# Last stage of a four-layer kernel: the running state and its product with the query in halves of two PSUM banks

## The chip, the cores and the metric

The kernel runs on one core of a Trainium2 chip. The metric is the device time of one execution in microseconds (us). Three runs of the kernel before gave 3492.67 to 3494.13 us, with a median of 3493.6 us. Engines are called PE (TensorE, the matrix engine), DVE (VectorE), ACT (ScalarE), POOL (GpSimd) and SP (SyncE, which issues DMAs here).

## The reference

Four layers follow one another on x of shape (16, 64, 32, 32), each as `x = x + layer(gn(x))`. Only the fourth is touched. For each image n its 65,536 values form a sequence s, and with A = 4 channels:

```python
q, k, v = in_proj_weight * x + in_proj_bias        # each n, s, A
q = softplus(q); k = softplus(k)
s = cumsum(k[:, :, :, None] * v[:, :, None, :], axis=1)
z = cumsum(k, axis=1)
numer = einsum('nsi,nsij->nsj', q, s)
denom = einsum('nsi,nsi->ns', q, z)[:, :, None]
y = numer / denom                                  # then shifted by one position
y = sum(hid_proj_weight * y, -1) + hid_proj_bias
y = sum(out_proj_weight * tanh(y), 1) + out_proj_bias
```

## The kernel before

The program has four stages, one per layer, that follow one another with a barrier between. The last is `layer3`. It takes one image after the other (B = 16, here called batches). The sequence of an image lies on 128 partitions by 512 columns (HALF), so one running sum over the sequence is a product with a lower triangle `tri` of ones within each column, plus what all columns before add up to, which is kept in `carry`.

Per batch there are five running sums, called terms: that of k (term 0, index A) and those of k*v_j for j = 0 to 3 (terms 1 to 4). Each term has four components i, and each component fills one PSUM bank of 512 float32 values per partition. So `p_state` has four banks, and it is there once; `p_sum` has two banks, `p_turn` and `p_out` one each, which makes all eight.

PE makes a term in `state(b, n)`: four products with `tri` (L1251), then four short ones (L1256) that add the carry of component i, which lies on its own 32 partitions ("lane"). The records of the trace have two entries for each such product of float32 values. DVE multiplies the four banks by the query in one operation, `times_query` (L1139), into one of two buffers `prod`. PE then transposes and adds the four components of `prod` into `p_sum` (`sum_terms`, L1271, sixteen transposes). From there DVE takes the reciprocal for term 0 (`denominator`, L1145) and `y` for the others (`divide`, L1151). After that the four products with the hidden weights (DVE L1161, PE L1282 and L1287), tanh on ACT (L1084), the gate on POOL (L1033) and the output (PE L1295 and L1301, one batch late) follow.

Each engine has an order written out by hand, in its own `main(b, u, left)`, and the engines meet in semaphores alone. PE's order in a batch is: `turn` of the next batch, `state` 0, `output` of the batch before, `state` 1, sum 0, `state` 2, sum 1, `state` 3, sum 2, `state` 4, sum 3, sum 4, then `totals` of the next batch (L1242, products with `pick`), then `hidden` four times. DVE puts work on the next batch's inputs between its five products: `project` (L1108), `lost_part` (L1113, written to `expo`), `relu_log` (L1117), `keys_x_values` (L1123, written to `kv`, a view of `xt`). ACT works on `expo` and `lift` (L1056 to L1064), POOL on the biases and the end of the softplus (L1015, L1019).

Two semaphores tie the terms. `state_ready` counts terms that PE has finished; DVE waits for it in `times_query`. `queried` counts products that DVE has finished; PE waits for it at the start of `state`, since the four banks are written anew, and in `sum_terms`. The batch before the first and the two last batches are written apart (`over_batches`); `left` is 0 in the last batch, which prepares no other.

Of the kernel before, what the change touches and what calls it, by code (L numbers as in the profile page):

```python
# [7 lines left out]
ALU = mybir.AluOpType  # L8
# [6 lines left out]
HALF = H * W // 2  # L15
# [869 lines left out]
def layer3(nc, xt, d, out, early, row_stats):  # L885


    A = ATT
    TERMS = A + 1
    LOCAL = TERMS + A  # L890
    LANE = 32
    tiles, early_in = early
    inw, inb = (tiles[name] for name in EARLY)
    with ExitStack() as ctx:
        def sb(name, shape, dt=F32):
            return ctx.enter_context(nc.sbuf_tensor(name + "_3", shape, dt))

        def pb(name, shape):
            return ctx.enter_context(nc.psum_tensor(name + "_3", shape, F32))

        def sem(name):
            return ctx.enter_context(nc.semaphore(name + "_3"))
# [6 lines left out]
        query = [sb(f"query{n}", [P, A, HALF]) for n in range(2)]  # L909
        expo, lift = sb("expo", [P, A, HALF]), sb("lift", [P, A, HALF])  # L910
        hidw = [sb(f"hidw{n}", [P, A, HALF]) for n in range(2)]
        prod = [sb(f"prod{n}", [P, A, HALF]) for n in range(2)]
# [3 lines left out]
        carry = sb("carry", [P, HALF + 1])  # L916
# [6 lines left out]
        p_state = pb("p_state", [P, A, HALF])  # L923
# [18 lines left out]
        state_ready = sem("state_ready"); queried = sem("queried"); summed = sem("summed")  # L942
# [5 lines left out]
        def known(b):  # L948
            return isinstance(b, int)
# [146 lines left out]
        def _(dve):  # L1096
            tt, stt = nc.vector.tensor_tensor, nc.vector.scalar_tensor_tensor
# [30 lines left out]
                                             op0=ALU.add, op1=ALU.bypass).then_inc(carry_ready, 1)  # L1128

            def times_query(b, u, n):  # L1130
                dve.wait_ge(state_ready, b * TERMS + (n + 1))
                if n == 0:
                    dve.wait_ge(soft, b * 2 + 2)
                if n < 2:
                    if not (known(b) and b == 0):
                        dve.wait_ge(hid_summed, b * A + (n - 1))
                else:
                    dve.wait_ge(summed, b * TERMS + (n - 1))
                tt(prod[(u + n) % 2][:], p_state[:], query[u][:], ALU.mult).then_inc(queried, 1)  # L1139

            def denominator(b, u):
                dve.wait_ge(summed, b * TERMS + 1)
# [20 lines left out]
            def main(b, u, left):  # L1163
                if left:
                    dve.wait_ge(x_turned, b + 2)
                    project(value, 2, v_scaled)
                times_query(b, u, 0)
                if left:
                    project(key, 1, k_scaled)
                    project(query[1 - u], 0, q_scaled)  # L1170
                times_query(b, u, 1)
                denominator(b, u)
                if left:
                    lost_part(b + 1, 0)
                times_query(b, u, 2)
                divide(b, u, 0)
                if left:
# [39 lines left out]
        def _(pe):  # L1217
# [13 lines left out]
            def term(j, i):  # L1231
                return key[:, i] if j == A else kv[:, j, i]
# [12 lines left out]

            def state(b, n):
                j = (n + A) % TERMS
                if not (known(b) and b == 0 and n == 0):
                    pe.wait_ge(queried, b * TERMS + n)
                for i in range(A):  # L1250
                    nc.tensor.matmul(p_state[:, i], tri[:], term(j, i), start=True, stop=False)  # L1251
                if n == 0:
                    pe.wait_ge(carry_ready, b + 1)
                for i in range(A):
                    lane = slice(i * LANE, (i + 1) * LANE)
                    last = nc.tensor.matmul(p_state[:, i], give[lane, j], carry[lane, 0:HALF], start=False, stop=True)  # L1256
                last.then_inc(state_ready, 1)

            def sum_terms(b, u, n):
                pe.wait_ge(queried, b * TERMS + (n + 1))  # L1260
                if n < 2:
                    if not (known(b) and b == 0):
                        pe.wait_ge(tanh_ready, b * A + (n - 1))
                elif n == 2:
                    pe.wait_ge(recip_ready, b + 1)
                else:
                    pe.wait_ge(y_ready, b * A + (n - 2))
                r = (u + n) % 2
                for k in range(4):
                    for i in range(A):  # L1270
                        last = nc.tensor.matmul(p_sum[r][:, k * P:(k + 1) * P], prod[r][:, i, k * P:(k + 1) * P], ident[:],  # L1271
                                                start=(i == 0), stop=(i == A - 1), is_transpose=True)
                last.then_inc(summed, 1)
# [31 lines left out]
            def main(b, u, left):  # L1305
                if left:
                    turn(b + 1)
                state(b, 0)
                if not (known(b) and b == 0):
                    output(b - 1)  # L1310
                for n in range(1, TERMS):
                    state(b, n)
                    sum_terms(b, u, n - 1)
                sum_terms(b, u, A)
                if left:
                    totals(b + 1, (A, 0, 1, 2, 3)).then_inc(totalled, 1)
                for a in range(A):
                    hidden(b, u, a)
# [110 lines left out]
```

## Time and profile before

| | |
|---|---|
| median of three runs | 3493.6 us (3492.67 to 3494.13) |
| the profiled execution | 3487.4 us, its span 3485.6 us |
| mean granted TensorE clock over the span | 0.722 of full |
| busy over the span: PE, DVE, ACT, POOL | 1637.2, 1815.1, 761.0, 1754.7 us |
| instructions | 32244 |

The last stage begins at about 2320 us of the span, with its batches from 2404 us on. Times of a row are in microseconds from the span's start, or durations. PE records show when products stream; the ends are modelled, so two groups that follow one another can overlap a little, and the distance between two starts is the better measure.

### The profile page before, as it was taken

Reading aid. Unit: us, or ns where it says so; the run is one execution under the profiler, and the core shown is the slowest. Engines: PE = TensorE matmul, PEld = TensorE weight load, DVE = VectorE, ACT = ScalarE, POOL = GpSimd, SP = SyncE. Lnnn points to the kernel's source line nnn. Section 1 sums busy time; section 2 is a strip of 40 time slices with the busy share of each in tenths; the row PEclk is TensorE's granted clock in tenths of the full one; section 3 lists DMA queues with packets and bytes.
Section 4 is the critical chain, followed back from the end, with each engine's and each line's share of the span. In section 5 each row is a group of like instructions: output and inputs, shape, how many; then the busy total and the mean of one; then the engine's idle time right before and its main releaser. Section 6 shows DMA issues by size and latency. Waiting matters only on the chain. (4 is left out here: it accounts for less than half of the span.)

```text
span 3485.6 us, 32244 instructions
## 1 busy us (share of the span) xinstructions
PE 1637.2 (47%) x12432; PEld 974.3 (28%) x12432; DVE 1815.1 (52%) x1717; ACT 761.0 (22%) x893; POOL 1754.7 (50%) x1342
## 2 busy tenths in 40 slices
PE   3666321321313123141231412634888878888887
PEld 2455210110101001010010100431455445445545
DVE  3222432441616326153262534555888887788885
ACT  3111211101102011010111100523433432343341
POOL 0000067576675757757577574044355445535542
PEclk9878655665656556565565655776989999998999
DMA  7999533232332323323233232221131122113212
GB/s 315 431 431 432 234 92 102 71 107 86 95 104 72 108 78 103 103 71 109 77 104 103 72 109 65 85 78 38 58 108 65 57 81 90 57 57 105 67 55 82
DMA packets 118313, 414.64 MB, mean 119 GB/s; under 512 B 24802, under 2 KB 59764, under 8 KB 101108
## 3 DMA queue, kind: packets, MB, share of 16 engines
q1 hardware_dynamic: 62964, 262.86, 19.9%
q0 software_dynamic: 55296, 151.07, 14.1%
q8 instruction: 35, 0.57, 0.1%
q14 instruction: 18, 0.15, 0.0%
HBM read 396.78 MB, written 17.05 MB: 119 GB/s over the span
## 5 line engine op out<-in xcount | busy, mean ns | idle before, releaser
L441 POOL DMA_INDIRECT gath<-table,idx x1152 | 1162.4, 1009 | 561.0 <-issue 347.3
L568 DVE TENSOR_TENSOR gath<-gath,p_stat 128x2304 f32<-128x2304 f32 x128 | 326.4, 2550 | 749.0 <-DMA gath<-table,idx 260.0
L646 PE MATMUL p_col<-ident,taps 128*128 128x128 f32 x512 | 116.4, 367 | 705.8 <-issue 533.8
L495 ACT ACTIVATE cols<-p_col 128x512 f32<-128x512 f32 x128 | 75.2, 597 | 1240.5 <-remote 827.8
L646 PEld LDWEIGHTS p_col<-ident,taps 128*128 128x128 f32 x512 | 77.8, 184 | 751.7 <-issue 744.5
L1251 PE MATMUL p_state<-xt,tri 128*128 128x512 f32 x512 | 257.4, 650 | 64.5 <-DVE prod L1139 64.5
L1019 POOL TENSOR_TENSOR query<-query,expo 128x2048 f32<-128x2048 f32 x16 | 102.1, 6382 | 334.7 <-DVE query L1117 334.7
L1139 DVE TENSOR_TENSOR prod<-p_state,query 128x2048 f32<-128x2048 f32 x80 | 183.0, 2288 | 127.5 <-PE p_state L1256 127.5
L595 PE MATMUL p_conv<-sides,wconv 128*32 128x512 f32 x192 | 70.4, 893 | 330.7 <-ACT rows L466 330.7
L1287 PE MATMUL p_sum<-ident,prod 128*128 128x128 f32 x1024 | 174.0, 341 | 104.0 <-DVE prod L1161 104.0
L1161 DVE TENSOR_TENSOR prod<-hidw,y 128x2048 f32<-128x2048 f32 x64 | 209.1, 3286 | 6.0 <-DMA hidw<-in_hidw 4.3
L622 PE MATMUL p_y<-cols,wreg 128*64 128x512 f32 x256 | 158.8, 778 | 108.5 <-issue 107.7
L422 POOL MEMSET zero<- 34x128 f32 x1 | 0.2, 198 | 409.5 <-POOLq L102 409.5
L286 PE MATMUL acc<-ring,win_a 128*32 128x128 f32 x3072 | 134.9, 342 | 145.4 <-DMA ring<-in_w 119.5
L1287 PEld LDWEIGHTS p_sum<-ident,prod 128*128 128x128 f32 x1024 | 155.3, 179 | 118.5 <-DVE prod L1161 118.3
L571 DVE TENSOR_TENSOR gath<-gath 128x1152 f32<-128x1152 f32 x128 | 173.8, 1358 | 4.4
L1033 POOL TENSOR_TENSOR gated<-gated,outw 128x512 f32<-128x512 f32 x64 | 143.2, 2254 | 62.2 <-ACT gated L1084 62.2
L1271 PE MATMUL p_sum<-ident,prod 128*128 128x128 f32 x1280 | 157.2, 276 | 8.9 <-DVE prod L1139 8.9
L1271 PEld LDWEIGHTS p_sum<-ident,prod 128*128 128x128 f32 x1280 | 138.4, 141 | 61.2 <-issue 53.6
L286 PEld LDWEIGHTS acc<-ring,win_a 128*32 128x32 f32 x3072 | 107.7, 137 | 167.3 <-DMA ring<-in_w 135.3
L1251 PEld LDWEIGHTS p_state<-xt,tri 128*128 128x128 f32 x512 | 99.7, 205 | 182.4 <-issue 105.7
L1123 DVE TENSOR_TENSOR xt<-key,value 128x2048 f32<-128x2048 f32 x64 | 143.3, 2281 | 4.6 <-POOL key L1019 4.6
(231 smaller groups left out, 2917.4 us busy)
## 6 DMA issues: line engine op xcount, KB each, us to landing
ring<-in_w SPq DMA_DIRECT2D x64, 2304.0 KB, 18.6
hidw<-in_hidw SPq DMA_DIRECT2D x64, 1024.0 KB, 4.9
gath<-table,idx POOLq DMA_INDIRECT x1152
table<-pix SPq DMA_DIRECT2D x64, 128.0 KB, 2.2
xt<-in_x SPq DMA_DIRECT2D x1, 4096.0 KB, 12.5
ring<-in_x SPq DMA_DIRECT2D x1, 4096.0 KB, 12.2
resid<-xt SPq DMA_DIRECT2D x32, 128.0 KB, 2.4
xlate<-resid SPq DMA_DIRECT2D x16, 256.0 KB, 3.0
```

The lines of the kernel that those rows point to most:

```text
L286: nc.tensor.matmul(acc[u][g * QUAD:(g + 1) * QUAD, h, q], pair.rearrange("p j b -> p (j b)"), wt[:, g, 4 * h + m], start=(q == 0 and m == ...
L441: nc.gpsimd.indirect_dma_start(out=gath[:, t % SLOTS, k].rearrange("p n c -> p (n c)"), out_offset=None, in_=tables[u], in_offset=bass.Ind ...
L568: tt(g, g, w, ALU.mult).then_inc(weighted, 1)
L571: tt(sides_of[:, :, 0], sides_of[:, :, 0], sides_of[:, :, 1], ALU.add).then_inc(halved, 1)
L622: last = nc.tensor.matmul(p_y[h * C:(h + 1) * C], wreg[:, k], cols[h][:, k].rearrange("p q x -> p (q x)"), start=(k == 0), stop=False)
L646: last = nc.tensor.transpose(p_col[t % 2][:, k], taps[:, t, 2 * k:2 * k + 2].rearrange("p k c -> p (k c)"), ident[:])
L1123: tt(kv[:, j], key[:], value[:, j:j + 1].to_broadcast([P, A, HALF]), ALU.mult).then_inc(kv_ready, 1)
L1139: tt(prod[(u + n) % 2][:], p_state[:], query[u][:], ALU.mult).then_inc(queried, 1)
L1161: tt(prod[(u + TERMS + a) % 2][:], hidw[a % 2][:], y[:], ALU.mult).then_inc(hid_scaled, 1)
L1251: nc.tensor.matmul(p_state[:, i], tri[:], term(j, i), start=True, stop=False)
L1271: last = nc.tensor.matmul(p_sum[r][:, k * P:(k + 1) * P], prod[r][:, i, k * P:(k + 1) * P], ident[:], start=(i == 0), stop=(i == A - 1), i ...
L1287: last = nc.tensor.matmul(p_sum[r][:, k * P:(k + 1) * P], prod[r][:, j, k * P:(k + 1) * P], ident[:], start=False, stop=(j == A - 1 and k ...
```

## The change

A term is made and used in two halves, g = 0 (banks 0 and 1) and g = 1 (banks 2 and 3). PE makes the two `tri` products and the two carry products of the first half, signals, and goes on to the second. DVE multiplies each half in an operation of its own and signals after each, so both semaphores count ten per batch and no longer five. PE may begin the first half of term n once DVE has read the first half of term n - 1, and `sum_terms` waits for both halves as it waited for the whole. No product is added or left out. On DVE the wait for the term is put behind the waits for `soft`, `hid_summed` or `summed`.

```diff
--- before.py
+++ after.py
@@ -1128,7 +1128,6 @@
                                              op0=ALU.add, op1=ALU.bypass).then_inc(carry_ready, 1)
 
             def times_query(b, u, n):
-                dve.wait_ge(state_ready, b * TERMS + (n + 1))
                 if n == 0:
                     dve.wait_ge(soft, b * 2 + 2)
                 if n < 2:
@@ -1136,7 +1135,10 @@
                         dve.wait_ge(hid_summed, b * A + (n - 1))
                 else:
                     dve.wait_ge(summed, b * TERMS + (n - 1))
-                tt(prod[(u + n) % 2][:], p_state[:], query[u][:], ALU.mult).then_inc(queried, 1)
+                for g in range(2):
+                    terms = slice(2 * g, 2 * g + 2)
+                    dve.wait_ge(state_ready, b * (2 * TERMS) + (2 * n + g + 1))
+                    tt(prod[(u + n) % 2][:, terms], p_state[:, terms], query[u][:, terms], ALU.mult).then_inc(queried, 1)
 
             def denominator(b, u):
                 dve.wait_ge(summed, b * TERMS + 1)
@@ -1245,19 +1247,20 @@
 
             def state(b, n):
                 j = (n + A) % TERMS
-                if not (known(b) and b == 0 and n == 0):
-                    pe.wait_ge(queried, b * TERMS + n)
-                for i in range(A):
-                    nc.tensor.matmul(p_state[:, i], tri[:], term(j, i), start=True, stop=False)
-                if n == 0:
-                    pe.wait_ge(carry_ready, b + 1)
-                for i in range(A):
-                    lane = slice(i * LANE, (i + 1) * LANE)
-                    last = nc.tensor.matmul(p_state[:, i], give[lane, j], carry[lane, 0:HALF], start=False, stop=True)
-                last.then_inc(state_ready, 1)
+                for g in range(2):
+                    if not (known(b) and b == 0 and n == 0):
+                        pe.wait_ge(queried, b * (2 * TERMS) + (2 * n - 1 + g))
+                    for i in range(2 * g, 2 * g + 2):
+                        nc.tensor.matmul(p_state[:, i], tri[:], term(j, i), start=True, stop=False)
+                    if n == 0 and g == 0:
+                        pe.wait_ge(carry_ready, b + 1)
+                    for i in range(2 * g, 2 * g + 2):
+                        lane = slice(i * LANE, (i + 1) * LANE)
+                        last = nc.tensor.matmul(p_state[:, i], give[lane, j], carry[lane, 0:HALF], start=False, stop=True)
+                    last.then_inc(state_ready, 1)
 
             def sum_terms(b, u, n):
-                pe.wait_ge(queried, b * TERMS + (n + 1))
+                pe.wait_ge(queried, b * (2 * TERMS) + (2 * n + 2))
                 if n < 2:
                     if not (known(b) and b == 0):
                         pe.wait_ge(tanh_ready, b * A + (n - 1))
```

On PE, here are terms 1 and 2 of a batch of the loop with the sum between them, in the kernel before (`xt` is the buffer of k*v, REGISTER_ALU computes the value that a wait is for):

```order
L1251 MATMUL p_state<-xt,tri 128x512 [waits queried_3]
L1251 MATMUL p_state<-xt,tri 128x512 x3
L1256 MATMUL p_state<-carry,give 128x512 x4
...
L1271 MATMUL p_sum_3<-ident,prod_3 128x128 [waits tanh_ready_3]
L1271 MATMUL p_sum_3<-ident,prod_3 128x128 x15
L1249 REGISTER_ALU
L1251 MATMUL p_state<-xt,tri 128x512 [waits queried_3]
L1251 MATMUL p_state<-xt,tri 128x512 x3
L1256 MATMUL p_state<-carry,give 128x512 x4
```

and the same place in the changed kernel:

```order
L1254 MATMUL p_state<-xt,tri 128x512 [waits queried_3]
L1254 MATMUL p_state<-xt,tri 128x512
L1259 MATMUL p_state<-carry,give 128x512 x2
L1252 REGISTER_ALU
L1254 MATMUL p_state<-xt,tri 128x512 [waits queried_3]
L1254 MATMUL p_state<-xt,tri 128x512
L1259 MATMUL p_state<-carry,give 128x512 x2
L1266 ISA [waits queried_3]
L1274 MATMUL p_sum_3<-ident,prod_3 128x128 [waits tanh_ready_3]
L1274 MATMUL p_sum_3<-ident,prod_3 128x128 x15
```

The runs of four `tri` products and four carry products have become two runs of two each, so PE goes from one shape to the other three times per term in place of once, and waits for DVE once per half.

On DVE, here is the place of products 1 and 2 in the kernel before, in the first batch:

```order
L1139 TENSOR_TENSOR prod_3<-p_state,query_3 128x2048 [waits state_ready_3]
L1145 RECIPROCAL recip<-p_sum_3 128x512 [waits summed_3]
L1113 SCALAR_TENSOR_TENSOR expo<-lift,expo 128x2048 [waits lifted_3]
L1139 TENSOR_TENSOR prod_3<-p_state,query_3 128x2048 [waits summed_3,state_ready_3]
L1151 TENSOR_TENSOR y<-p_sum_3,recip 128x512 [waits recip_ready_3,summed_3]
```

and in the changed kernel:

```order
L1141 TENSOR_TENSOR prod_3<-p_state,query_3 128x1024 [waits state_ready_3] x2
L1147 RECIPROCAL recip<-p_sum_3 128x512 [waits summed_3]
L1113 SCALAR_TENSOR_TENSOR expo<-lift,expo 128x2048 [waits lifted_3]
L1141 TENSOR_TENSOR prod_3<-p_state,query_3 128x1024 [waits state_ready_3,summed_3]
L1141 TENSOR_TENSOR prod_3<-p_state,query_3 128x1024 [waits state_ready_3]
L1153 TENSOR_TENSOR y<-p_sum_3,recip 128x512 [waits recip_ready_3,summed_3]
```

Each product of 2048 elements per partition is now two of 1024; nothing has moved past anything else.

## Rows read from the trace of the kernel before

**Rows 1.** Waits in the last stage: us in total, times, longest.
```profile
DVE prod L1139 <- PE p_state L1256: 127.5, 50, 7.2
...
PE p_state L1251 <- DVE prod L1139: 64.5, 49, 4.6
```
**Rows 2.** Timeline, DVE and POOL, one batch: start, us, operation, count, [idle before].
```profile
2821.25 2.29 DVE L1139 TENSOR_TENSOR prod<-p_state,query 128x2048 f32<-128x2048 f32 x1 [2.35 <-PE p_state L1256]
...
2828.90 2.29 DVE L1139 TENSOR_TENSOR prod<-p_state,query 128x2048 f32<-128x2048 f32 x1 [0.97 <-PE p_state L1256]
...
2831.11 3.35 DVE L1145 RECIPROCAL recip<-p_sum 128x512 f32<-128x512 f32 x1
...
2836.22 2.29 DVE L1113 SCALAR_TENSOR_TENSOR expo<-lift,expo 128x2048 f32<-128x2048 f32 x1 [1.76 <-ACT lift L1060]
...
2840.63 0.68 DVE L1151 TENSOR_TENSOR y<-p_sum,recip 128x512 f32<-128x512 f32 x1
...
2841.23 2.28 DVE L1117 SCALAR_TENSOR_TENSOR key<-key,lift 128x2048 f32<-128x2048 f32 x1
2843.58 4.52 POOL L1019 TENSOR_TENSOR key<-key,expo 128x2048 f32<-128x2048 f32 x1 [8.73 <-DVE key L1117]
...
2845.61 2.29 DVE L1139 TENSOR_TENSOR prod<-p_state,query 128x2048 f32<-128x2048 f32 x1 [2.10 <-PE p_state L1256]
2847.81 0.68 DVE L1151 TENSOR_TENSOR y<-p_sum,recip 128x512 f32<-128x512 f32 x1
...
2852.81 2.28 DVE L1139 TENSOR_TENSOR prod<-p_state,query 128x2048 f32<-128x2048 f32 x1
```
**Rows 3.** Timeline, PE, the same batch.
```profile
2816.41 3.60 PE L1251 MATMUL p_state<-key,tri 128*128 128x512 f32 x8
2819.94 1.14 PE L1256 MATMUL p_state<-carry,give 32*128 32x512 f32 x8
2821.01 1.13 PE L1295 MATMUL p_out<-xlate,ident 128*128 128x512 f32 x2
...
2824.16 3.60 PE L1251 MATMUL p_state<-xt,tri 128*128 128x512 f32 x8
...
2831.24 3.70 PE L1251 MATMUL p_state<-xt,tri 128*128 128x512 f32 x8 [0.52 <-DVE prod L1139]
...
2840.77 3.70 PE L1251 MATMUL p_state<-xt,tri 128*128 128x512 f32 x8 [2.85 <-DVE prod L1139]
```
**Rows 4.** Timeline, PE and DVE, term 3 of two other batches.
```profile
2907.04 5.40 PE L1251 MATMUL p_state<-xt,tri 128*128 128x512 f32 x8 [2.96 <-DVE prod L1139]
...
2913.57 2.29 DVE L1139 TENSOR_TENSOR prod<-p_state,query 128x2048 f32<-128x2048 f32 x1 [3.79 <-PE p_state L1256]
...
3381.25 5.40 PE L1251 MATMUL p_state<-xt,tri 128*128 128x512 f32 x8 [2.76 <-DVE prod L1139]
```
**Rows 5.** Timeline, PE's weight loads, from `tri` to the carries.
```profile
2885.16 0.19 PEld L1251 LDWEIGHTS p_state<-key,tri 128*128 128x128 f32 x1 [0.24 <-issue]
2886.11 0.31 PEld L1256 LDWEIGHTS p_state<-carry,give 32*128 32x128 f32 x8 [0.76 <-issue]
```
**Rows 6.** Timeline, PE, third layer: products side by side in pairs.
```profile
2315.08 1.04 PE L855 MATMUL p_b<-ident,mod 128*64 128x128 f32 x16
```
**Rows 7.** Timeline, PE, sums 3 and 4 and the totals of another batch.
```profile
2920.62 1.97 PE L1271 MATMUL p_sum<-ident,prod 128*128 128x128 f32 x16
2923.19 1.96 PE L1271 MATMUL p_sum<-ident,prod 128*128 128x128 f32 x16 [0.61 <-DVE prod L1139]
2925.08 1.07 PE L1242 MATMUL p_turn<-key,pick 128*32 128x512 f32 x8
2925.97 3.62 PE L1242 MATMUL p_turn<-xt,pick 128*32 128x512 f32 x32
```
**Rows 8.** Timeline, PE, the last batch: term 0 and sum 4.
```profile
3424.38 3.60 PE L1251 MATMUL p_state<-key,tri 128*128 128x512 f32 x8
...
3460.76 1.96 PE L1271 MATMUL p_sum<-ident,prod 128*128 128x128 f32 x16 [0.52 <-DVE prod L1139]
```

## The prediction

> **What bounds the kernel now.** Only the last stage changes, so the page's shares over the whole span say little, and I read that stage alone. First its waits: DVE waits 127.5 us in all for `p_state`, and PE waits 64.5 us for DVE's products [rows 1]. So the two engines wait for each other, which is where the change acts.
>
> Then one batch in order of time, on DVE and on PE. I count from the start of its `state(b,0)` on PE at 2816.41. DVE's products 0, 1, 3 and 4 start at 4.84, 12.49, 29.20 and 36.40, and a product takes 2.20 us until the next operation (2845.61 to 2847.81) [rows 2]. Behind the last one the batch goes on in a fixed order of DVE work up to the next turn, and moves along as a whole. So what counts for a batch is when the fifth product gives way to the next operation: 36.40 + 2.20 = 38.60.
>
> On PE one term costs 3.53 us for its eight records with `tri` (2816.41 to 2819.94) and 1.07 us for the carries (to 2821.01), together 4.60; `output` takes 3.15 (to 2824.16) [rows 3]. PE then idles 0.52 us before term 2 and 2.85 us before term 3. The second is the dear one. In 13 of the 15 batches that prepare another, term 3 looks as in [rows 4]: after 2.76 to 2.96 us of idle (more in the first batch) its eight records take 5.40 us in place of 3.70, and DVE waits 3.79 us for it in place of 2.10 [rows 2, 3]. That is TensorE at the lower of its two clocks, 1.2 GHz, for a part of the stretch. Either way the difference is 1.7 us, and nothing behind takes it up.
>
> **The change, part by part.**
>
> *The carries lose half of their company.* A carry product uses 32 rows of the array, and the four of a term run side by side: eight records in 1.14 us [rows 3]. Their loads take 0.31 us, after 0.76 us in which nothing was loaded, against 0.24 between the `tri` loads [rows 5]. After the change two run together, twice per term. No row shows a pair of 32-row products. Bounds: 0.54 us if time follows their number, 1.07 if a pair takes as long as four. The nearest row is a pair of another shape: sixteen records of 128 columns, eight products in pairs, take 1.04 us, 0.26 a pair at most [rows 6]; four strips side by side with 512 columns take 0.89 (2925.08 to 2925.97) [rows 7]. Four times the columns, about four times the time, whether two or four run together: a set costs what one product costs. I take 1.07.
>
> The Trainium skill ("TensorE: Matmul & The Clock Gate", Part 3, "Measured speedup vs the span model") gives tiles side by side the time of one matmul plus about 4 ns per further tile. By it, as an estimate, a pair costs 1.06 and the sum would end about 1 us lower; by the bound of 0.54 it would end some 20 us lower. The rows above side with the page, but none of them has this shape.
>
> *The `tri` products go in pairs too.* Four records at 0.43 (0.19 of load and 0.24 between loads [rows 5]) are 1.72. The first pair bears the turn to 32 rows: 3.53 less twice 1.72 is 0.09, so 1.81. The second stands behind a carry, so its first load is bare: 0.10 more, the difference between 3.60 and 3.70 in [rows 3]. It costs 1.91. A term is then 1.81 + 1.07 + 1.91 + 1.07 = 5.86 in place of 4.60.
>
> *The two semaphores.* PE may write half of a term as soon as DVE has read these two banks. DVE may read the first half 1.81 + 1.14 + 0.07 = 3.02 after the term starts, the second 5.86 + 0.07 + 0.07 = 6.00 after: a group's last record reaches 0.07 over the next start (1.14 against 1.07), and DVE starts 0.07 behind it (2824.16 + 4.67 against 2828.90 [rows 2, 3]).
>
> *Two halves on DVE.* 80 products become 160. Two operations on 512 elements lie 0.60 apart (2840.63 to 2841.23 [rows 2]); a product of 2048 takes 2.20. Four times 512 in four instructions would be 2.40, so each instruction more costs 0.07: a half costs 1.14, both 2.27.
>
> *The new batch.* PE: term 0 to 5.86, `output` to 9.01, term 1 to 14.87. A sum of sixteen transposes takes 1.80 (2923.19 to 2925.08 is 1.89 with a turn of 0.09 [rows 7]): to 16.67. Term 2 to 22.53, sum 1 to 24.33, term 3 to 30.19, sum 2 to 31.99, term 4 to 37.85, sum 3 to 39.65. Does DVE hold it up? Product 0 is over at 6.00 + 1.14 = 7.14 (now 7.04), product 1 at 16.15. The reciprocal starts when sum 0 is in, at 16.67 + 0.16 + 0.07 = 16.90 (now 14.70), and takes 3.27, so `expo` starts at 20.17 rather than 19.81: the 1.76 us that it now waits for ACT cover most of it [rows 2]. It takes 2.20, and the halves of product 2 start at 22.37 and 23.51, the first over before PE asks for its banks at 24.33. So **PE has no idle from 0 to the end of sum 3**: the 2.85 or 2.96 us are gone, and with them what goes ahead of the slow stretch.
>
> But PE now leads. `y` 1 needs sum 2, printed 1.97 long [rows 7]: 30.19 + 1.97 + 0.07 = 32.23, now 31.40. Five us later (2847.81 to 2852.81, its own 0.60 and two `kv`) DVE starts the first half of product 4, at 37.23, the second at 38.37 (ready at 31.99 + 6.00 = 37.99), the next operation at 39.51. Against 38.60 that is **0.91 later per batch**. POOL's `key`, 4.52 us and now started 2.35 after `relu_log` starts [rows 2], would be in at about 25.2 + 2.35 + 4.52 = 32.1, `kv` wants it at 32.8: just hidden.
>
> *The sum.* Fifteen batches at +0.91: +13.6. The last batch, in which PE alone sets the pace, gets to its last sum at 3460.76 - 3424.38 = 36.38 [rows 8] and will at 39.65: +3.3. Thirteen slow stretches of 1.7 gone: -22.1. Together -5.2 us. The profiled execution's 3487.4 would become 3482.2; it lies 6.2 below the median of the runs, and against that the forecast is 3493.6 - 5.2 = **3488.4 us**. A measurement of this kernel can tell about 0.2%, 7 us, from no change, so this lies just within: a gain of clock and a loss of PE time of like size.
>
> **The rivals.**
>
> *A, faster: pairs cost half.* With 0.54 a pair, a term is 4.80. The fifth product then waits through POOL's `key`, not for PE, and is over some 0.1 us sooner than now (-2 in all), the last batch gains about 2, and the 22 stay saved, since term 3 would start after some 2.0 us of idle, less than any that now goes ahead of a slow one: -26, **3467.6 us**. For it: the short loads in [rows 5]. Against it: rows 6 and 7.
>
> *B, slower: the slow stretch stays.* Then the new PE work is paid and nothing comes back: 13.6 + 3.3, **3510.5 us**. Its place is the `tri` records of term 3, or another term's in its stead; each that runs slow costs 1.7, so from 8 of 13 on the kernel is slower by over 7 us. For it: PE still does 1.8 us of transposes between two terms, and they might not hold the clock. Against it: after two sums with only 0.61 us of idle, over 4 us of transposes, the eight records with `pick` still start 0.89 us before the next group, the fast rate [rows 7]. What went ahead of the slow ones was idle time, and that is gone.
> The Trainium skill ("TensorE: Matmul & The Clock Gate", Part 4) says that the full clock does not engage for transposes, which do not count as busy in the same way; by that, B would come true. The trace does not agree: sixteen transposes in 1.89 us are 0.12 each, the full rate.
>
> *C, faster: the turns hide.* If the added turn (0.09) and bare load (0.10) of a term lie beside something, four terms give 0.8 us per batch and the last as much: -12.8 more, -18, **3475.6 us**. For it, only that such small terms are read off modelled ends; against it, that loads are seen to stop for 0.76 us at every turn [rows 5].
>
> **How the numbers follow.** The main case has 0.66, and its own range is 3482 to 3496: 0.1 us in each of four terms moves the sum by 6. A has 0.07, C 0.06, B, wholly or in part, 0.16; 0.05 is for something slower that I don't see. Of the main case 0.25 lies under 3486.6 (with A and C 0.38 for faster by over 0.2%) and 0.41 within 0.2%; slower by over 0.2% has 0.21. The range leaves out the far halves of A and B: 3474 to 3506.
>
> **What would show it.** In the changed kernel's profile: terms of 5.8 to 5.9 us, carries of 1.0 to 1.1 per pair; PE's waits for products near zero in a batch, no 5.40 at term 3; batches 0.8 us closer together than those in which term 3 is slow now, 0.9 further apart than the other two; DVE's waits for `p_state` not gone but spread over the halves. Wrong would be: pairs of carries near 0.5; slow `tri` records in most batches; a DVE that waits for POOL before `kv`.

## The result, and the profile after

The changed kernel is slower: 3502.12 us in the median of 11 runs, against 3491.17 us for eleven runs of the kernel before beside it. The ratio is 1.0037, with a 95% interval from 1.0020 to 1.0054. Forecast were 3488.4 us and a ratio of 0.9985. The direction was wrong. 3502.1 us lies outside the main case's own range (3482 to 3496) and inside the wide one (3474 to 3506). Single runs of the changed kernel lie further apart (3483 to 3516 us) than those of the kernel before (3473 to 3497).

The profiled execution took 3501.7 us (span 3499.8). Not all of the 14.2 us between the two spans is the change's. The first `value` of the batches, the last thing ahead of the changed code, starts at 2411.54 us in place of 2404.88, so 6.7 us were lost in layers that the change doesn't touch. From there to the end it is 1088.3 us in place of 1080.7: **+7.5 us**. I compare this length below and call it the stage. It comes from one profiled execution of each kernel.

The forecast's picture of one batch holds. This is the timeline of PE in the changed kernel, terms 3 and 4 of a batch that starts at 2822.12 (start, us, operation, count, [idle before]):

```profile
2844.60 1.97 PE L1274 MATMUL p_sum<-ident,prod 128*128 128x128 f32 x16
2846.40 1.88 PE L1254 MATMUL p_state<-xt,tri 128*128 128x512 f32 x4
2848.21 1.13 PE L1259 MATMUL p_state<-carry,give 32*128 32x512 f32 x4
2849.27 1.98 PE L1254 MATMUL p_state<-xt,tri 128*128 128x512 f32 x4
2851.18 1.13 PE L1259 MATMUL p_state<-carry,give 32*128 32x512 f32 x4
2852.24 1.96 PE L1274 MATMUL p_sum<-ident,prod 128*128 128x128 f32 x16
2854.04 1.88 PE L1254 MATMUL p_state<-xt,tri 128*128 128x512 f32 x4
```

A term takes 5.84 us (2846.40 to 2852.24), a pair of carries 1.06, a sum 1.80, and no idle time stands in front of any group. Against [rows 3, 4], the 2.85 us of idle and the 5.40 us of term 3 are gone. Slow `tri` records are left in the first batch alone: at its start (3.49 us for four; the kernel before has 5.66 for eight there), and at its term 3, where PE still idles 3.24 us and the first half then takes 2.96 in place of 1.88 us, its carries 1.80 in place of 1.13.

DVE in the same batch:

```profile
2852.36 1.23 DVE L1141 TENSOR_TENSOR prod<-p_state,query 128x1024 f32<-128x1024 f32 x1 [1.62 <-PE p_state L1259]
2854.25 0.69 DVE L1153 TENSOR_TENSOR y<-p_sum,recip 128x512 f32<-128x512 f32 x1 [0.66 <-PE p_sum L1274]
2854.85 4.48 DVE L1123 TENSOR_TENSOR xt<-key,value 128x2048 f32<-128x2048 f32 x2
2859.25 2.35 DVE L1141 TENSOR_TENSOR prod<-p_state,query 128x1024 f32<-128x1024 f32 x2
2861.52 2.28 DVE L1123 TENSOR_TENSOR xt<-key,value 128x2048 f32<-128x2048 f32 x1
...
2890.59 2.29 DVE L1108 TENSOR_TENSOR value<-inw_early,p_turn 128x2048 f32<-128x2048 f32 x1 [4.23 <-PE p_turn L1230]
```

`y` 1 starts at 32.13 from the batch's start (forecast 32.23) and the operation behind the fifth product at 39.40 (39.51). The rest is where the forecast fails: the last row. DVE waits 4.23 us for the turned input (I call this the wait at the turn), and 4.17 to 4.28 us in 12 of the 14 batches behind the first. In the kernel before it was 2.92 to 3.19 us. In the view of waits (us in total, times, longest) it stands in both kernels, before and after:

```profile
DVE value L1108 <- PE p_turn L1228: 44.2, 15, 3.2
```

```profile
DVE value L1108 <- PE p_turn L1230: 58.1, 15, 4.3
```

This is what PE does ahead of it, first in the kernel before, then in the changed one (sixteen transposes with the products of the hidden weights, L1287 and L1290, are the rows to look at):

```profile
2933.67 3.00 PE L1287 MATMUL p_sum<-ident,prod 128*128 128x128 f32 x16 [2.69 <-DVE prod L1161]
2936.46 1.06 PE L1282 MATMUL p_sum<-ident,hidb 128*128 128x128 f32 x4
2938.07 1.97 PE L1287 MATMUL p_sum<-ident,prod 128*128 128x128 f32 x16 [0.55 <-DVE prod L1161]
...
2944.60 3.63 PE L1287 MATMUL p_sum<-ident,prod 128*128 128x128 f32 x16 [4.12 <-DVE prod L1161]
2948.04 0.62 PE L1282 MATMUL p_sum<-ident,hidb 128*128 128x128 f32 x4
2948.50 1.91 PE L1287 MATMUL p_sum<-ident,prod 128*128 128x128 f32 x16
```

```profile
2872.21 3.46 PE L1290 MATMUL p_sum<-ident,prod 128*128 128x128 f32 x16 [2.69 <-DVE prod L1163]
2875.51 0.60 PE L1285 MATMUL p_sum<-ident,hidb 128*128 128x128 f32 x4
2876.61 1.97 PE L1290 MATMUL p_sum<-ident,prod 128*128 128x128 f32 x16 [0.50 <-DVE prod L1163]
...
2883.14 3.67 PE L1290 MATMUL p_sum<-ident,prod 128*128 128x128 f32 x16 [4.12 <-DVE prod L1163]
2886.60 1.06 PE L1285 MATMUL p_sum<-ident,hidb 128*128 128x128 f32 x4
2887.46 2.66 PE L1290 MATMUL p_sum<-ident,prod 128*128 128x128 f32 x16
```

Before, after an idle time of 4.12 us the third set ran slow (3.63) and the bias transposes and the fourth set, which DVE's wait at the turn hangs on, were fast again (0.62 and 1.91). After, the slow stretch reaches over the bias (1.06) into the fourth set (2.66). The idle time ahead is the same 4.12 us. This is one batch: in eight of the fifteen batches before, the fourth set is slow in part too (2.06 to 2.66 us), but there the third takes less (2.43 to 3.11). What counts is the sum of third set, bias and fourth set. It is 6.0 to 6.3 us in all fifteen batches before, and 7.3 to 7.5 in all but the first two after. The view by windows gives the granted clock of that last piece, for the changed kernel and for the kernel before (columns: stretch, its length, busy time of PE, of its loads, of DVE, ACT and POOL, granted clock, DMA share, GB/s):

```profile
2886.20:2890.00 3.80, 3.80 (x24) 3.80 (x23) 0.16 (x1) 0.60 (x1) 2.56 (x2) 0.63 0.93 336
```

```profile
2948.00:2950.70 2.70, 2.70 (x27) 2.70 (x26) 0.00 (x0) 0.85 (x2) 2.21 (x2) 0.99 0.92 303
```

0.63 against 0.99: for most of that piece TensorE ran at the lower of its two clocks, 1.2 GHz. The DMA share is 0.93 and 0.92, so the transfers don't make the difference.

The bill of the stage, by the starts of the fifteen `value`: the fourteen intervals took 952.3 us before and 956.9 after, +4.6. Twelve of the thirteen slow stretches lie in them, so the forecast has 14 x 0.91 - 12 x 1.7 = -7.7. What is left, the last two batches, took 128.4 and 131.4: +3.0, where the forecast has 0.91 - 1.7 + 3.3 = +2.5. The fourteen waits at the turn that end these intervals add up to 42.9 us before and 56.9 after, **+14.0**. Without them the intervals are 9.4 us shorter. So the waits are the whole difference between +7.5 and -5.2, and 1 us more. One batch shows it by itself: the second, whose wait at the end is 3.12 us (3.07 before), took 67.16 us in place of 68.12, close to the 0.8 less that the forecast has.

Two theories then: **M**, the slow stretch of PE moved from term 3 to the hidden products, where it lies on the path of the batch; and **P**, the loss is PE's added work and nothing else.

### The profile page after: what moved, and what is told of

It is laid out like the page before. It is cut to its first block and busy times, and to the rows that moved or that the text cites. A ratio compares the mean times of both kernels' runs of the same rounds, so it can differ in the third digit from the quotient of the medians.

```text
span 3499.8 us, 32438 instructions
## 1 busy us (share of the span) xinstructions
PE 1692.5 (48%) x12432; PEld 981.0 (28%) x12432; DVE 1823.4 (52%) x1797; ACT 761.2 (22%) x893; POOL 1760.6 (50%) x1342
## 5 line engine op out<-in xcount | busy, mean ns | idle before, releaser
L1141 DVE TENSOR_TENSOR prod<-p_state,query 128x1024 f32<-128x1024 f32 x160 | 192.5, 1219 | 114.6 <-PE p_state L1259 114.6
L1254 PE MATMUL p_state<-xt,tri 128*128 128x512 f32 x512 | 248.6, 608 | 3.2 <-DVE prod L1141 3.2
L595 PE MATMUL p_conv<-sides,wconv 128*32 128x512 f32 x192 | 78.2, 981 | 333.3 <-ACT rows L466 333.3
L1290 PE MATMUL p_sum<-ident,prod 128*128 128x128 f32 x1024 | 182.5, 353 | 115.1 <-DVE prod L1163 115.1
L1290 PEld LDWEIGHTS p_sum<-ident,prod 128*128 128x128 f32 x1024 | 167.5, 189 | 126.9 <-DVE prod L1163 126.9
L622 PE MATMUL p_y<-cols,wreg 128*64 128x512 f32 x256 | 151.5, 747 | 106.3 <-issue 105.6
L1259 PE MATMUL p_state<-carry,give 32*128 32x512 f32 x640 | 181.0, 642 | 0.0
L1274 PEld LDWEIGHTS p_sum<-ident,prod 128*128 128x128 f32 x1280 | 138.4, 141 | 49.6 <-issue 48.5
L1019 POOL TENSOR_TENSOR key<-key,expo 128x2048 f32<-128x2048 f32 x16 | 72.5, 4529 | 146.0 <-DVE key L1117 146.0
```

Of the source, the lines that this page charges most:

```text
L1019: tt(part[:], part[:], expo[:], ALU.subtract).then_inc(soft, 1)
L1141: tt(prod[(u + n) % 2][:, terms], p_state[:, terms], query[u][:, terms], ALU.mult).then_inc(queried, 1)
```

## The experiments

All ratios are to runs of the kernel before on the same chip. "Stage" is the length from the first `value` of the batches to the end of the span; that of the kernel before is 1080.7 us. "Waits" are the fourteen waits at the turn behind the first batch's, 42.9 us in the kernel before.

| kernel | ratio, 95% interval | stage, us | waits, us |
|---|---|---|---|
| changed | 1.0037, 1.0020 to 1.0054 | 1088.3 | 56.9 |
| changed, again | one run | 1089.2 | 59.0 |
| e1, carries of four | 0.9949, 0.9932 to 0.9966 | 1060.8 | 42.6 |
| e2, PE's halves only | 1.0109, 1.0092 to 1.0126 | 1119.2 | 42.1 |
| e3, DVE's halves only | 1.0020, 1.0008 to 1.0033 | 1087.1 | 42.4 |
| e4, changed, PE kept busy | 0.9966, 0.9957 to 0.9976 | 1066.9 | 35.0 |
| e5, before, hidden phase kept busy | 0.9952, 0.9935 to 0.9969 | 1065.6 | 35.0 |
| e8, before, term 3 kept busy | 0.9938, 0.9921 to 0.9954 | 1064.2 | 44.4 |
| e6, e1 with hidden phase kept busy | 0.9918, 0.9902 to 0.9935 | 1054.5 | 35.0 |
| e9, before, both kept busy | 0.9937, 0.9919 to 0.9956 | 1053.1 | 35.0 |
| e10, e1 with both kept busy | 0.9916, 0.9896 to 0.9935 | 1048.5 | 35.0 |

The changed kernel again, e5, e8 and e6 ran on a chip on which the kernel before takes 3247.1 us; its earlier layers are quicker there. Their ratios are therefore to a smaller base. The kernel before was not traced there; that stages can be compared across the chips rests on the changed kernel's two, 1088.3 and 1089.2 us.

**The parts of the change.** `e1` keeps what the change is for and not its price: the halves wait and release as in the change, but the carries stay together.

```diff
+                for g in range(2):
+                    if not (known(b) and b == 0 and n == 0):
+                        pe.wait_ge(queried, b * (2 * TERMS) + (2 * n - 1 + g))
+                    for i in range(2 * g, 2 * g + 2):
+                        nc.tensor.matmul(p_state[:, i], tri[:], term(j, i), start=True, stop=False)
                 if n == 0:
                     pe.wait_ge(carry_ready, b + 1)
                 for i in range(A):
```

> The change without its price: DVE multiplies and releases in halves, PE begins the tri products of half g once that half is free, but the four carry products stay together and one signal ends a term. Theory M (the slow stretch of PE moved from term 3 to the products with the hidden weights, where it lies on the path): terms cost 4.6 to 4.7 us; term 3 starts about 1 us earlier; at most 17 us faster than the kernel before, of which part is given back in the hidden phase (DVE's wait at the turn over 3.1 us), so -5 to -17 us. Theory P (the loss is PE's added work and nothing else): 15 to 20 us faster, hidden phase unchanged.

Measured: 3474.99 us against 3491.52, -16.5 us, and the stage 19.9 us shorter. The timeline of PE:

```profile
2843.40 1.97 PE L1274 MATMUL p_sum<-ident,prod 128*128 128x128 f32 x16
2848.00 3.70 PE L1254 MATMUL p_state<-xt,tri 128*128 128x512 f32 x8 [2.63 <-DVE prod L1141]
2851.63 1.14 PE L1259 MATMUL p_state<-carry,give 32*128 32x512 f32 x8
...
2914.06 5.40 PE L1254 MATMUL p_state<-xt,tri 128*128 128x512 f32 x8 [2.73 <-DVE prod L1141]
```

Term 3 is slow in 7 of 15 batches now and no longer in 13, though PE idles nearly as long before it. The gain is at the far end of what M allowed and the near one of P's. M's sign, a wait at the turn over 3.1 us, did not come: it is 2.71 to 3.07 us, and once 4.30. The changed kernel's stage is 27.5 us longer than that of e1. That is not the price of the pairs of carries alone: 14.3 us of it are the waits at the turn. In the other 13.2 us the pairs' added work of PE stands against e1's seven slow terms 3.

`e2` takes PE's order of the change alone: pairs of `tri` and carry products, one signal and one release per term.

```diff
+                for g in range(2):
+                    for i in range(2 * g, 2 * g + 2):
+                        nc.tensor.matmul(p_state[:, i], tri[:], term(j, i), start=True, stop=False)
...
+                    for i in range(2 * g, 2 * g + 2):
+                        lane = slice(i * LANE, (i + 1) * LANE)
+                        last = nc.tensor.matmul(p_state[:, i], give[lane, j], carry[lane, 0:HALF], start=False, stop=True)
```

> PE's order of the change (pairs of tri and carry products), with one signal per term and whole products on DVE. A term costs 5.86 us and PE and DVE alternate: the fifth product is over about 3.9 us later per batch. Theory M: no idle over 0.7 us is left before term 3, so no slow tri records there, but DVE's wait at the turn is about 4.2 us as in the changed kernel: +50 to +60 us against the kernel before. Theory P: wait at the turn 3.1, +40 to +47 us.

Measured: 3530.75 us, +39.2, the stage +38.5. No slow `tri` records at term 3, as both have it. But DVE's wait at the turn goes back and forth between 2.74 and 3.18 us (the first three are 2.50, 3.07 and 4.18):

```profile
2834.57 2.29 DVE L1108 TENSOR_TENSOR value<-inw_early,p_turn 128x2048 f32<-128x2048 f32 x1 [2.74 <-PE p_turn L1228]
...
2904.76 2.29 DVE L1108 TENSOR_TENSOR value<-inw_early,p_turn 128x2048 f32<-128x2048 f32 x1 [3.17 <-PE p_turn L1228]
```

M missed here as I had put it, and P's figure is near. The hidden phase is not slower wherever term 3 is fast. So a dense state phase is not enough for the long wait; my reading is that what decides is where in the hidden phase the slow stretches fall.

`e3` splits DVE's product and nothing else; PE waits for both halves.

```diff
-                tt(prod[(u + n) % 2][:], p_state[:], query[u][:], ALU.mult).then_inc(queried, 1)
+                for g in range(2):
+                    terms = slice(2 * g, 2 * g + 2)
+                    tt(prod[(u + n) % 2][:, terms], p_state[:, terms], query[u][:, terms], ALU.mult).then_inc(queried, 1)
```

> Only DVE's product in two operations; PE waits for both and works as before. Both theories: 0.07 us per product, three to five of them on the path of a batch: +3 to +5 us, slow tri records at term 3 in most batches, wait at the turn 3.1 us. If this alone costs over 8 us, the halves on DVE are dearer than the rows say and explain the loss.

Measured: ratio 1.0020 (medians 4.9 us apart), the stage +6.4, a little over what was expected. All 15 batches have a slow term 3 in place of 13, which at 1.7 us each is about half of it. The wait at the turn is 3.01 to 3.07 us, and batches are 68.2 to 68.3 us apart, as in the changed kernel.

**The clock by itself.** `e4` is the changed kernel with PE kept busy where it idles in the hidden phase. The products go to `p_state`, which is free then, and nothing reads them.

```diff
+                for f in range((2, 0, 3, 0)[a]):
+                    nc.tensor.matmul(p_state[:, f], tri[:], term(A, f), start=True, stop=True)
                 pe.wait_ge(hid_scaled, b * A + (a + 1))
```

> The changed kernel, and PE makes two further products of 512 columns into p_state (free then, results unused) while it waits for the first product with the hidden weights, and three while it waits for the third. Theory M: the sixteen transposes of the hidden products take 1.97 us everywhere in place of 3.4 to 3.7, DVE's wait at the turn falls from 4.23 to 2.5 to 2.8 us, batches from 68.27 to 66.6 to 66.9 us: about 20 us faster than the changed kernel, 5 to 12 us faster than the kernel before. Theory P: the extra products change nothing or cost time; wait at the turn stays above 4 us.

Measured: 3478.91 us, 12.6 less than the kernel before and 23 less than the changed one's median above, the stage 1066.9 in place of 1088.3 us. PE does more and the kernel is quicker. The timeline of PE and DVE:

```profile
2864.40 2.74 PE L1288 MATMUL p_state<-key,tri 128*128 128x512 f32 x6
2868.69 1.97 PE L1292 MATMUL p_sum<-ident,prod 128*128 128x128 f32 x16 [1.55 <-DVE prod L1163]
2870.49 0.60 PE L1285 MATMUL p_sum<-ident,hidb 128*128 128x128 f32 x4
2871.97 1.97 PE L1292 MATMUL p_sum<-ident,prod 128*128 128x128 f32 x16 [0.88 <-DVE prod L1163]
```

```profile
2874.41 2.29 DVE L1108 TENSOR_TENSOR value<-inw_early,p_turn 128x2048 f32<-128x2048 f32 x1 [2.50 <-PE p_turn L1230]
```

The third and fourth set take 1.97 us each, and the wait at the turn is 2.49 to 2.50 us in all fourteen batches behind the first, which are 66.45 to 66.56 us apart. The fourteen waits are 21.9 us less than in the changed kernel, and the stage is 21.4 us less. The granted clock over this hidden phase, in the view by windows with the columns as above, is full:

```profile
2857.80:2873.80 16.00, 11.57 (x83) 9.31 (x84) 14.12 (x5) 1.79 (x3) 13.82 (x4) 1.00 0.61 209
```

In every other batch the second set is still slow (3.26 us in the next batch), but PE has 1.55 us of idle time behind it that takes this up. This is the experiment that tells the theories apart: with the terms as they are in the change, what differs is the extra products and the clock of the hidden phase. P is out as the whole story.

Did the changed kernel's 4.23 us come by chance? It ran once more, on the other chip.

> The changed kernel unaltered, to see whether its batches settle in the same way in another execution. If theory M is right and the layout of slow stretches belongs to the length of a batch, DVE's wait at the turn is again about 4.2 us and the batches 68.2 to 68.3 us apart, whatever the start of the stage is. If it was chance, other waits show, between 2.7 and 4.3.

Measured: 3258.54 us against a median of 3247.08, +11.5 us; waits at the turn of 4.15 to 4.26 us in all fourteen behind the first batch's (1.27), batches 68.22 to 68.27 us apart behind the first, the stage 1089.2 us. So the layout is no chance of one execution.

`e5` is the kernel before with e4's lines.

> The kernel before with the same extra products in the hidden phase. Theory M: slow stretches leave the hidden phase, wait at the turn 2.5 us in place of 3.07, term 3 stays slow or not as before (idle of 2.9 us before it is still there): 5 to 12 us faster than before. If the extra products helped for another reason than the clock, the sixteen transposes would still show 3.4 us and more.

Measured: ratio 0.9952, -15.1 us, more than expected. The wait at the turn is 2.49 to 2.50 in every batch behind the first, which makes some 8 us; term 3 is slow in 9 of 15, not 13, which makes about 7 more. So an extra gain came from a place that was not touched. That term 3's fate also depends on when it comes is how I read it, not shown by itself.

`e8` is the step of my forecast by itself: only the idle time before term 3 is filled, with two products into `p_out`, whose content has been read by then.

```diff
+                    if n == 3:
+                        if not (known(b) and b == 0):
+                            pe.wait_ge(o_ready, b)
+                        for f in range(2):
+                            nc.tensor.matmul(p_out[:], tri[:], outw[:, f], start=True, stop=True)
                     state(b, n)
```

> The kernel before, with two extra products of 512 columns into p_out (read out by then, results unused) in the idle time before term 3. It tests the step of my prediction by itself: filling that idle time alone takes the slow tri records away (3.70 in place of 5.40 in all batches). By the prediction as written, 22 us less and nothing behind changes: -20 to -24 us. By theory M a part comes back in the hidden phase, where DVE's wait at the turn rises over 3.1 in some or all batches: 0 to -15 us.

Measured: -20.1 us, the edge of what the forecast's theory said and beyond what M said. Term 3 is fast in 14 batches of 15. The hidden phase becomes uneven: waits at the turn of 2.50 (three times), 2.75 to 3.07 (eight times), and 4.16, 4.37 and 4.32 us. One of those, in the timeline of PE:

```profile
2559.01 3.68 PE L1287 MATMUL p_sum<-ident,prod 128*128 128x128 f32 x16 [4.13 <-DVE prod L1161]
2562.48 1.06 PE L1282 MATMUL p_sum<-ident,hidb 128*128 128x128 f32 x4
2563.33 2.79 PE L1287 MATMUL p_sum<-ident,prod 128*128 128x128 f32 x16
...
2587.73 1.88 PE L1316 MATMUL p_out<-outw,tri 128*128 128x512 f32 x4
2590.74 3.70 PE L1251 MATMUL p_state<-xt,tri 128*128 128x512 f32 x8 [1.13 <-DVE prod L1139]
```

It is the same pattern as in the changed kernel (1.06 and then 2.79), in a kernel that has none of its edits. Over its batches the gain and the loss at the turn nearly cancel (44.4 us in all against 42.9), which is why the forecast's step held here and not in the changed kernel, whose batches all have the costly pattern.

**Faster versions.** `e6` joins e1 and e4's lines, `e9` is the kernel before with both fillings, `e10` is e1 with both.

> e1_carries_of_four with the extra products in the hidden phase. Theory M: what the halves gain without the pairs of carries, and no slow stretch at the turn: wait at the turn 2.5 us, 5 to 10 us faster than e1_carries_of_four, 22 to 27 us faster than the kernel before. Term 3 may still be slow in batches, since PE idles 2.7 us before it.

> The kernel before with the extra products in both places, before term 3 and in the hidden phase. Theory M: no slow record of PE is left in a batch; wait at the turn 2.5 us in all, tri records of term 3 3.70 in all, batches 65.5 to 65.7 us apart, the last stage about 33 us shorter than the kernel before's 1080.7 us. If each filling only pushes the slow stretch to another place, about -16 us as each alone.

> e1_carries_of_four with the extra products in both places. Theory M: term 3 starts 1 us earlier than in e9 and nothing is slow, but kv waits for POOL's key instead, so a batch is only 0 to 0.3 us shorter than e9's; with the last batch's 2 to 3 us, 3 to 7 us faster than e9, 36 to 40 us faster than the kernel before.

Measured: e6 -26.8 us, its stage 6.3 us shorter than e1's; e9 -23.3 us, with 2.49 to 2.50 at every turn behind the first, one slow term 3 (in the first batch) and, between the first interval and the last, batches of 65.7 to 65.9 us; e10 3462.86 us against 3491.62, -28.8. Both fell short. The stage is 27.6 us shorter in e9, forecast 33; e10 was to be 36 to 40 us faster. I can't place what is missing. e9's "no slow record is left" missed too: its second hidden set is slow in 7 of 15 batches (2.39 to 3.61 us), with idle time behind it that takes most of this up. e10 is 5.4 us ahead of e9, as expected. The two fillings of e9 together save as much as the sum of their single savings in the stage less 4 (15.1 and 16.5 give 31.6), so neither undoes the other. e10 has the shortest stage and beats both kernels; by the ratios it can't be told from e6 (0.9916 and 0.9918).

## Why the prediction was wrong

- *A pair of carries costs as much as four: 1.07 us.* Right: 1.06. Rival A (0.54) is out. It also agrees with the rule of the Trainium skill ("TensorE: Matmul & The Clock Gate", Part 3) on tiles side by side, which had given 1.06.
- *A term costs 5.86 in place of 4.60.* Right: 5.84. Rival C, hidden turns, is out.
- *PE leads and the fifth product is over 0.91 us later.* Right: 39.40 against a forecast of 39.51, so 0.80 later. POOL's `key` stayed hidden.
- *The last batch, +3.3.* Right: from its first `tri` record to the bias transposes behind its last sum PE takes 41.31 us in place of 38.18, +3.1. To the end of the span it is +2.6, for the kernel before has slow hidden products there.
- *The slow stretch of term 3 goes.* Right but for the first batch: one of 13 is left, and no other term got one. Rival B in its wording is out. Its 3510.5 us lie nearer to the measured time than the main case's, but by luck: its slow stretch was to stay in the terms. The rule of the Trainium skill ("TensorE: Matmul & The Clock Gate", Part 4) that transposes don't bring the full clock does not hold here either: in e4 a whole hidden phase of transposes with some products between runs at a granted clock of 1.00. And in the last batch of the kernel before PE does nothing but transposes from 3460.76 to 3479.01 us; the granted clock is 0.64 in one piece and 1.00 in a later one:

```profile
3466.10:3469.00 2.90, 2.83 (x17) 2.83 (x18) 2.21 (x2) 0.00 (x0) 0.00 (x0) 0.64 0.65 184
3473.50:3479.00 5.50, 4.20 (x36) 3.96 (x37) 2.30 (x2) 0.60 (x1) 3.18 (x2) 1.00 0.02 7
```

- *"Behind the last one the batch goes on in a fixed order of DVE work up to the next turn, and moves along as a whole."* This is the step that failed. The DVE work does, but at its end stands a wait for PE, and how long PE needs there depends on its clock. The wait had 2.92 to 3.19 us in the kernel before. The forecast has no term for it, which makes it a constant without a reason. It became 4.17 to 4.28 us in 12 of 14 batches: 14.0 us more in all, which covers the whole miss (+7.5 for the stage, against -5.2). The sets behind it were on the path already: DVE waited 44.2 us for them in the kernel before. e4 shows that their clock is the cause; e8 shows the costly pattern without the change's edits.

What stays open: why the slow stretch falls where it does, why the changed kernel settles at 68.27 us, and why e2 alternates. The length of a batch does not fix the layout: e3 has the same 68.2 to 68.3 us with a slow term 3 and a wait of 3.0 us at the turn. The batches of the changed kernel are 67.2 us apart once (2482.22 to 2549.38), and from then on 68.2 to 68.3, with the same pattern at every turn. I have not made an experiment that moves a batch's length by small steps. Nor is it shown whence the 3 us come by which the medians differ more than the stages do (11 against 7.5 to 8.5); the earlier layers are the same code.

## What to carry to other kernels

Where PE has idle time in a loop and another engine waits for it, its clock can be a part of the critical path: look at every set of products behind an idle time, and ask what a slow one would cost if it fell one set later. A wait that one kernel has in every batch is not a constant of the next. Products that use 32 rows of the array each should stay together in fours, for a pair takes as long (1.06 against 1.07 us); a split of the work for an earlier hand-over should go around them (e1). And a few products without use in PE's idle time are a cheap probe of what the clock costs, here also a gain of 0.6% (e9).

## What was not expected of the hardware

- The length of a batch locks: 68.22 to 68.27 us for eleven batches in a row, and 68.26 on another chip whose earlier layers take 240 us less. What each kernel locks at: e4 has 66.53 to 66.56, e3 the same as the changed kernel (68.23 to 68.31), e2 two lengths in turn (69.75 and 70.19).
- Two batches with nearly the same idle time before term 3 (2.63 and 2.73 us in e1) have it fast and slow; in the kernel before, the same 2.85 us goes ahead of a slow one (at 2568.26 us) and a fast one (at 2840.77 us). The idle time alone doesn't tell; e5 changed how often term 3 is slow, 13 to 9 of 15, with edits only in the hidden phase (one trace of each).
- A piece of idle time half as long is not free of it either: the second set of e4 has only 2.0 us before it and is slow in every other batch (3.26 us in one).
